# Moving four pairs of row gathers ahead on GpSimd, and one PSUM bank's clearing ahead on VectorE, at the start of a second transformer layer

## The reference, cut to what matters

```python
x = x + attention0(layernorm(x), ctx, ctx, mask, ...)          # first layer
h = layernorm(x)
x = x + mean of 2 shared experts(h) + sum of the top 2 of 8 routed experts(h), weighted
# second layer: 16 heads of 16 features, no mask
q, k, v = layernorm(x) @ Wq.T, ctx @ Wk.T, ctx @ Wv.T
x = x + (softmax(q k^T / 4) v) @ Wo.T
x = x + layernorm(x) @ W.T + b + (layernorm(x) @ V_r) @ C.T
```

## Time and profile before

| | |
|---|---|
| median of three executions | 735.87 us |
| the profiled execution | 739.63 us |
| its span in the profile | 737.8 us |
| granted TensorE clock | 0.999 of full speed |
| busy share of TensorE, VectorE, ScalarE, GpSimd | 98%, 64%, 42%, 37% |
| dense stage of the second layer | from 520.1 us to about 545 us |
| blocks 0 to 3 | from about 545 us to about 588 us |

### The profile page before, as it was taken

The page is one execution under the profiler, slowest core; times in us unless marked ns, Lnnn a source line. Parts: engine busy times, 40 slices in busy tenths (PEclk is TensorE's granted clock), DMA queues, the critical chain, the costliest instruction groups (busy, mean ns, idle before and its releaser), DMA issues.

```text
span 737.8 us, 15558 instructions
## 1 busy us (share of the span) xinstructions
PE 719.7 (98%) x5770; PEld 557.1 (76%) x5770; DVE 469.1 (64%) x1074; ACT 311.6 (42%) x559; POOL 270.6 (37%) x318
## 2 busy tenths in 40 slices
PE   8999999999999999999999999999998999999997
PEld 6676668666876575799999998989775667777775
DVE  4678674657465679644444655728677878788725
ACT  1224221421142122155555554645245855565562
POOL 3985333523310534402200514224734435305050
PEclk9999999999999999999999999999999999999999
DMA  9899944741521495823453422454877675754101
GB/s 246 203 299 267 235 141 134 213 124 42 178 80 53 152 381 191 284 62 86 120 138 94 125 78 87 132 144 129 247 222 190 179 193 158 210 161 123 34 3 51
DMA packets 73516, 114.10 MB, mean 155 GB/s; under 512 B 15153, under 2 KB 59794, under 8 KB 71522
## 3 DMA queue, kind: packets, MB, share of 16 engines
q1 hardware_dynamic: 61984, 85.93, 40.9%
q0 software_dynamic: 6160, 15.67, 6.9%
q10 hardware_dynamic: 5298, 11.51, 5.6%
HBM read 84.27 MB, written 28.41 MB: 153 GB/s over the span
## 4 chain that ended last, share of the span: by engine, by line
PE 89%; DVE 3%; POOL 2%; DMA 2%; ACT 2%; issue 1%; ACTq 0%; DVEq 0%; SPq 0%
PE ps L1587 17%; PE ps L1204 12%; PE ps L1596 8%; PE ps L1224 6%; PE ps L2345 5%; PE ps L2374 5%; PE ps L1243 5%; PE ps L2365 5%; PE ps L1255 4%; PE ps L1172 3%; PE ps L2338 3%; PE ps L1144 2%; PE ps L2319 2%; DVE mxh L1992 2%; PE ps L1179 2%; PE ps L2274 2%
## 5 line engine op out<-in xcount | busy, mean ns | idle before, releaser
L1992 DVE TENSOR_REDUCE mxh<-ps 112x2 f32<-112x750 f32 x128 | 115.1, 933 | 32.9 <-PE ps L2345 29.2
L1587 PE MATMUL ps<-rowsT,w 128*128 128x128 f32 x1120 | 130.9, 275 | 0.0
L1587 PEld LDWEIGHTS ps<-rowsT,w 128*128 128x128 f32 x1120 | 128.0, 192 | 0.2
L2198 ACT ACTIVATE d_pT<-ps 125x448 f32<-125x448 f32 x192 | 91.8, 549 | 45.3 <-PE ps L2365 43.7
L1541 ACT ACTIVATE w<-rw 128x1024 f32 x70 | 73.8, 1055 | 69.6 <-PE ps L1587 48.0
L1204 PE MATMUL ps<-x1T,sw 128*128 128x448 f32 x256 | 101.2, 540 | 0.0
L1204 PEld LDWEIGHTS ps<-x1T,sw 128*128 128x128 f32 x256 | 47.5, 190 | 38.6 <-issue 35.1
L1480 POOL DMA_DIRECT2D yscr<-y x35 | 19.7, 563 | 151.4 <-DVE y L1514 151.4
L1596 PE MATMUL ps<-rw,h 128*128 x280 | 66.4, 380 | 0.0
L2345 PE MATMUL ps<-kst,qst 96*112 96x375 bf16 x256 | 58.6, 332 | 1.7 <-DVE mxh L1992 1.7
L995 ACT ACTIVATE silu<-ps,sb 128x448 f32<-128x448 f32 x32 | 20.3, 633 | 87.0 <-PE ps L1204 81.4
(11 more groups left out here) (272 smaller groups left out, 1201.4 us busy)
## 6 DMA issues: line engine op xcount, KB each, us to landing
kst<-kscr SPq DMA_DIRECT2D x39, 378.0 KB, 5.2
rw<-in_rw SPq DMA_DIRECT2D x24, 512.0 KB
kscr<-ka SPq DMA_DIRECT2D x16, 567.0 KB
cT<-in_ctx_t SPq DMA_DIRECT2D x17, 378.0 KB, 4.6
ctxT<-in_ctx_t SPq DMA_DIRECT2D x16, 378.0 KB
ctxn<-in_ctx SPq DMA_DIRECT2D x16, 336.0 KB
rows<-xg SPq DMA_DIRECT2D x35, 128.0 KB
rb<-in_rb SPq DMA_DIRECT2D x35, 128.0 KB
```

What stands on the lines that cost most here:

```text
L1587: last = mm(bank[1 + 2 * q + k][:, block], w12[:, k, c, block], rowsT[:, q, c * P:(c + 1) * P], start=c == 0, stop=c == C - 1)
L1992: V.tensor_reduce(mxh[:, b % 2, 2 * g:2 * g + 2], ps[0:S, p:p + 2, 0:K], axis=AX_X, op=ALU.max).then_inc(s["s_max"], 1)
L2198: A(pT[:, q % 2, k, :], bank[4 + k][0:KC, 0:QUAD * S], ACT.Exp).then_inc(s["p_ready"], 1)
```

## The change

In GpSimd's stream the gathers of group 3 come earlier: those of its batch elements 0 and 1 (four indirect DMAs) right behind the filling of the key copies 1 and 2 and of the ones column, those of 2 and 3 right behind the splitting of the queries; their waits for `p_ready` go. The filling of key copy 3 and of the second query buffer comes behind them, then `parted` of 2 and 3.

In VectorE's stream bank 7 is cleared between the sixth and the seventh maximum of batch element 1 and no longer behind its parting. It waits for the values of batch element 13 (which lay in bank 7) and for the copy of the first transposed maxima. So that nothing else is in bank 7 by then, the third chunk of the values of batch element 15 goes to bank 5. TensorE waits before this chunk for the copies of element 14's values, and in block 0 for all copies before the second chunk of the transposed scores, since that is in bank 5 too; before, it was before the third.

```diff
@@ gpsimd
+        i = NG - 1
         ones_below(pool, 1)
         ones_below(pool, 2)
-        ones_below(pool, 3)
         pool.memset(va[:, :, :, :, HD:HD + 1], 1.0).then_inc(s["va_ready"], 1)
-        pool.wait_ge(s["va_ready"], 2)
-        zeros_below(pool, 1)
+        for j in range(G // 2):
+            gather(pool, i, j)
         pool.wait_ge(s["m_ready"], 4)
         split_queries(pool, EARLY - 1)
         split_rest(pool, EARLY - 1)
-        i = NG - 1
-        for j in range(G):
-            if j % 2:
-                parted(pool, j // 2 + 2)
-            pool.wait_ge(s["p_ready"], (2 * j + 2) * NKC)
+        for j in range(G // 2, G):
             gather(pool, i, j)
+        ones_below(pool, 3)
+        pool.wait_ge(s["va_ready"], 2)
+        zeros_below(pool, 1)
+        parted(pool, 2)
+        parted(pool, 3)
@@ vector
-        for g in range(8):
+        for g in range(6):
+            maximum(1, g)
+
+        v.wait_ge(s["mT_ready"], 1)
+        v.wait_ge(s["v_ready"], B - 2)
+        V.memset(bank[7][:], 0.0).then_inc(s["clear"], 1)
+        for g in range(6, 8):
             maximum(1, g)
         parted(v, 1)
-
-        v.wait_ge(s["v_ready"], B)
-        V.memset(bank[7][:], 0.0).then_inc(s["clear"], 1)
@@ late_banks
+        if b == B - 1:
+            return 6, 5
@@ tensor
+        t.wait_ge(s["v_ready"], B - 1)
         late_values(B - 1, range(2, NKC))
-        t.wait_ge(s["v_ready"], B - 1)
...
-            transposed(b, 0, range(2))
+            transposed(b, 0, range(1 if b == 0 else 2))
             if b == 0:
                 score(0)
                 score(1)
                 t.wait_ge(s["v_ready"], B)
-            transposed(b, 0, range(2, NKC))
+            transposed(b, 0, range(1 if b == 0 else 2, NKC))
```

## The result

The change makes the kernel slower. Six executions of the changed kernel have a median of 740.90 us (740.48 to 742.16), six of the kernel before beside them 735.81 us (734.67 to 737.73). The ratio is 1.0069 with an interval of 1.0057 to 1.008, which is +5.1 us. I had forecast 734.2 us with a range up to 737.7, so both the sign and the range were wrong. The profiled execution of the changed kernel took 740.48 us, with a span of 738.7 us and a granted clock of 0.994.

What follows compares the result with a forecast made beforehand. TensorE, busy 98% of the span, was taken as the bound, with time won only where it waits. Bank -0.5, gathers -2.6, lateness +1.4 gave -1.7 us off the 735.9 median: 734.2 us, range 732.0 to 737.7.

Steps and rivals of the forecast that it cites:

- The fillings: GpSimd behind the moved gathers: key copy 3 filled 545.5 to 548.15, query buffer 548.2 to 551.3, no delay.
- second run of gathers: GpSimd's four gather issues behind the splitting of the queries, placed at 540.75 to 545.45.
- rival C: Fillings hold up the casts of element 1's parting, ending it 4.8 us late: +1.7, 737.6 us; chance 0.15.
- 2.6: Gain in us from moving gathers out of blocks 0 and 1: 1.2 plus 1.43; bounds 1.5 and 3.0.
- Rival D: Gaps in blocks 0 and 1 aren't the gathers' and stay; only the clearing's 0.5 us is won: 735.4; chance 0.09.
- rival A: No late signals beside the gathers in their new place: -3.3 us, 732.6; chance 0.26.
- Lateness in the new place: Dense stage, seventh maximum of element 1 late beside the moved gathers: 1.4 us lost, bounds 0 and 2.09.
- B: Signals late in both moved runs of gathers, +1.3 and +2.1 against -3.1: +0.3, 736.2 us; chance 0.12.
- Bank 7: Clearing moved into VectorE's wait ahead of the seventh maximum: gain 0.48 us, bounds 0 and 0.6.
- late loads: Moved gathers' traffic delaying loads TensorE needs in the dense stage: counted nothing, 0.5 us at the worst.
- first run of gathers: GpSimd's four gather issues in the dense stage, placed at 528.05 to 532.8; lateness taken as 0, 1.3 at worst.

Runs made afterwards that it cites:

- e2: Changed kernel with the fillings of key copy 3 and query buffer waiting for VectorE's parting of element 1: 735.19 us beside 739.95 for the kernel before.
- e4: Changed kernel, fillings left in place, the parting's casts replaced by a two-input maximum of the value with itself: 736.28 us, ratio 0.9944 to the kernel before.
- e14: Changed kernel with only key copy 3's filling beside the parting, the query buffer's waiting for it: 737.92 us beside 735.59 for the kernel before.
- e15: Kernel before with only the two fillings moved beside the parting of element 1; gathers, clearing and banks stay: 741.95 us beside 735.59.
- e13: Kernel before, unchanged, run again for a profile in session 4: 736.0 us beside 735.59.
- e8: Changed kernel with eight added zero-product matmuls in TensorE's gap ahead of the transposed maxima: 740.94 us beside 739.20 for the kernel before.
- e6: Changed kernel, unchanged, run again in session 2: 741.74 us beside 739.20 for the kernel before.
- e10: Kernel before with only the first pair of gathers (element 12) moved earlier, from block 0 to behind the queries' splitting: 737.92 us beside 739.37.
- e9: e2 with GpSimd's four waits for exponentials kept in blocks 0 and 1, without gathers there: 735.62 us, ratio 0.9948 to the kernel before.
- e5: Kernel before with only GpSimd's part changed, fillings behind the parting as in e2, clearing and banks as before: 735.87 us beside 739.20.
- e16: e2's kernel again, in session 5: 735.54 us beside 735.71 for the kernel before.
- e12: e2's kernel again, in session 3: 735.69 us, ratio 0.995 to the kernel before.
- e3: Kernel before with only the bank part (earlier clearing of bank 7, chunk to bank 5, TensorE's waits): 739.03 us beside 739.95.
- e17: e3's kernel again, in session 5: 735.18 us, ratio 0.9991 to the kernel before.
- e11: Kernel before, unchanged, run again for a profile in session 3: 739.53 us, ratio 1.0002.
- e18: Changed kernel, unchanged, run again in session 5: 740.73 us, ratio 1.0068 to the kernel before.

## Why the prediction was wrong

**The fillings.** The step that failed is the sentence on what follows the second run of gathers: "Filling key copy 3: 545.5 to 548.15. Filling the query buffer (3.08 us): 548.2 to 551.3. Then the parting of element 2 ...: no delay". It costs the fillings at nothing on GpSimd's own stream, and VectorE's casts beside them were left to rival C with a chance of 0.15. C was right in mechanism and nearly in its length: it had the parting 4.8 us late, the two casts took 4.46 us more, and TensorE's gap is 4.46. The filling of key copy 3 starts at 544.12 where I had put it at 545.5; 1.2 us of this is the whole dense stage, which is earlier in this profile (last pair of maxima at 543.04, before at 544.27), so it meets the casts as C had it. e2, e4, e14 and e15 show the mechanism from four sides. I had held the second cast of the earlier trace rows against C (0.57 us beside a running GpSimd instruction, against 1.12 beside an addition) and said that 16 elements are few. Size is no protection: a cast of 0.17 us waited for the filling's end. The quick cast of the earlier trace rows was no chance, though: the profile of the kernel before has four such casts that start beside this GpSimd instruction on int32 numbers, with 0.55, 0.57, 0.59 and 0.81 us, and 0.55 to 0.56 is what the cast takes with GpSimd idle; e13 repeats them to 0.02 us. Why these are not held to the end was not tried. GpSimd runs another kind of instruction there, and its rows are none for a filling. The rule of the Trainium skill that I had beside C (SBUF — State Buffer, Who interferes with whom: VectorE in a two-port mode and GpSimd take the shared ports for a whole instruction) agrees with the casts' 1.91 and 2.89 us here, each to its filling's end. No row shows whether these casts run in such a mode. The same section of the Trainium skill says that an instruction of VectorE with two inputs in SBUF is in the way only of a GpSimd instruction that reads SBUF, not of one that only writes; e4 agrees, with 0.17 and 0.18 us beside a filling. The row that I let outweigh the rule was of a different operation.

**The clock.** No term of the sum had it, nor had C. Behind a gap of 4.46 us TensorE ran at 0.50 for about five microseconds of work, which costs 1.6 to 1.9 us in block 0 beside e2 and at most 2.67 (e8 against e6). C took its 4.8 us and let 0.5 and 2.6 be won back; with the clock its 737.6 would have been 739.2 to 740.3. The 2.6 was not there to win in the result's session, as the next paragraph shows; the clock left out and this gain counted in both made C too low against 740.9.

**The gathers.** "I take the gathers for the cause of the lateness, by coincidence in time only" was right: e10 ties the gap of block 0 to its own pair, e9 clears GpSimd's waits, and e5 measures 3.3 us for the part, more than the 2.6 of the sum and its upper bound of 3.0. Rival D falls where the gaps exist. What was wrong is what I subtracted it from: "Taken off the median: 735.9 - 1.7". The profiled execution was at 739.63 us, 3.8 over the median. I said so and did not ask where those 3.8 us lay. Most of them lay beside the gathers, in the very time that I then counted as gain: against blocks without late signals (block 0 of e10 with 9.75 us, blocks 1 and 2 of e13 with 9.00 and 9.42) the blocks 0, 1 and 2 of the earlier trace rows are 1.36, 1.61 and 0.35 us longer, 3.3 in all. Sessions 1 to 3, with gaps, have the kernel before at 739.2 to 739.95, sessions 4 and 5 at 735.6 to 735.7, and e13's profile from such a session has none of them. The median already stood without the lateness, so 0 was to be had, and e16 (ratio 0.9996) measures just that. Against a time of 739.6, rival A's -3.3 would have been near without the fillings: e2 measured -4.8 us in session 1 and -3.7 in session 3.

**Lateness in the new place.** The +1.4 us did not come. In the result's profile no bias add beside the experts' gathers is late either, so that profile can't test it. But e2 in session 1, where such adds stand up to 5.95 us behind, has the last two maxima on time and 735.19 us. So rival A was right of those maxima, and B is out. Block 0 is not quite free of it: e4, e5 and e12, all with the gathers early, have 0.61 to 0.65 us of idle time there (last section).

**Bank 7.** As predicted in place and nearly in size: the clearing stands at 542.56, ahead of the last pair of maxima, at no cost; the gap of 0.70 us is gone (e3, e17), and e3 and e17 gain 0.9 and 0.5 us, both with intervals that reach no change. The forecast was 0.48.

**The account of +5.1 us.** Beside e13, profiled in a session like the result's, the changed kernel's transposed maxima stand at 550.26 against 546.61, at 561.57 against 557.90 and at 570.58 against 566.90: +3.65, +3.67, +3.68, and the spans differ by 3.8 (738.7 and 734.9). That is the idle time of 4.46 in the place of 0.70, less 0.1. Both executions have the low clock in block 0. Over the medians there are 1.3 us more. It fits that all three profiles of the changed kernel that I have show the clock at 0.50 behind the gap, but only one of the kernel before's three, and e17's execution without it has block 0 in 9.68 us (545.98 to 555.66) against e13's 11.29. The times on record point the same way: of the 50 executions of the kernel before in sessions 4 and 5, seven, e13's profiled one among them, have a granted clock of 0.996 over the span and a median of 736.76 us, the other 43 have 0.998 or more and 735.62 us. Only e13's profile shows in which block the clock was low, so this last part is argued and not shown.

## What to carry to other kernels

Before GpSimd work is moved, look at what VectorE runs beside the new place: a cast of 0.17 us from SBUF to SBUF waited for the end of every filling it met, and if TensorE waits for that cast the clock charges its own price on top. When the profiled execution differs from the timed median, find the difference in the rows first; a gap that only the profiled execution has is no gain. And try each part of a mixed change alone: here one part gained nothing or 3 us, one about half a microsecond that no run shows clear of the noise, and one lost 5.

## What was unexpected of the hardware

- Signals from TensorE to VectorE and ScalarE come up to 2.2 us late (5.95 against 3.77 in e2) beside indirect DMAs in some sessions and not in others, with the same kernel: 739.2 to 739.95 us on three chips, 735.6 to 735.8 us in the three other sessions. The profile of the earlier trace rows is of the late kind and the three timed executions beside it are not; whether it was taken on another chip is not on record. Within a session it is stable, and e11's gaps repeat those of the earlier trace rows to 0.04 us. Whether it belongs to the chip or to something else in the session stays open.
- The clock fell behind idle times of 0.70 and 0.31 us in e13 (0.50 from 549 to 551 us) and did not behind the same two in e11. What decides was not tried.
- e16's profile (737.73 us, against its median of 735.54) has 1.65 us of idle time ahead of four score matmuls of block 0, and e12's has 0.65 at the same place; e4 and e5 have 0.65 and 0.61 there, e2, e9 and e17 nothing. No gather is issued in these microseconds, and only versions with the gathers moved early show it. The cause is open:

```profile
554.40 0.85 PE L2352 MATMUL ps<-kst,qst 96*112 96x375 bf16 x4 [1.65 <-issue]
```

```profile
552.66 0.85 PE L2352 MATMUL ps<-kst,qst 96*112 96x375 bf16 x4 [0.65 <-DVE mxh L1994]
```

- TensorE waited for a context load in the dense stage, 1.46 us in e18 and 0.37 in e12. The prediction had put late loads there at nothing, 0.5 us at the worst; both are versions with the first run of gathers in this stage, and none of the seven profiles with that run in its old place has such a wait. Two cases in eleven such profiles do not show that the gathers cause it, and a single profile can carry an event that the median does not.
